# Encoding of the experts and their gates and decoders: from two turns of a loop to one written-out pipeline of 16 steps

## The reference, cut to what matters

```python
h = _ln(relu(x @ ew1 + eb1) @ ew2 + eb2, eg, ebeta)      # encoding
qkv = h @ aiw + aib                                      # encoding
...                                                      # attention, output projection,
hf = _lstm_dir(h, wif, whf, bf)                          # LSTM forwards and backwards
mem = concatenate([hf, hb])
gate_s = sigmoid(relu(mem @ sw1 + sb1) @ sw2 + sb2)      # gates
gate_t = tanh(relu(mem @ tw1 + tb1) @ tw2 + tb2)
g = gate_s * gate_t
out_e = _ln(relu(g @ dw1 + db1) @ dw2 + db2, dg, dbeta)  # decoder
...
out = einsum("ebsd,bse->bsd", outs, softmax(x @ router_w + router_b))
```

## Time and profile before

| | us |
|---|---|
| median of 3 runs | 5326.97 (5326.27 to 5326.97) |
| the profiled execution | 5325.8 |
| its span, first to last instruction | 5324.0 |
| encoding, from the memset of `evx` to the last store of `qk` | 289.35 to 622.77 |
| gates and decoders, from the first load to the last sum | 4773.99 to 5236.68 |
| PE busy, share of the span | 94% |
| DVE / ACT / POOL busy | 77% / 45% / 22% |

### The profile page before, as it was taken

The page is one execution under the profiler, slowest core; times in us unless marked ns, Lnnn a source line. Parts: engine busy times, 40 slices in busy tenths (PEclk is TensorE's granted clock), DMA queues, the critical chain, the costliest instruction groups (busy, mean ns, idle before and its releaser), DMA issues. The chain is left out here.

```text
span 5324.0 us, 258931 instructions
## 1 busy us (share of the span) xinstructions
PE 5025.1 (94%) x108704; PEld 3528.2 (66%) x108704; DVE 4120.1 (77%) x19249; ACT 2395.4 (45%) x8347; POOL 1150.2 (22%) x5133
## 2 busy tenths in 40 slices
PE   7978799999999996999999999999999999989895
PEld 4654433333333335999999999999999999974442
DVE  3855666666666658999999999999999999972225
ACT  2633465555555544444444444444444444433332
POOL 0000011111111101333333333333333333320000
PEclk9988899999999998999999999999999999999997
DMA  0023544545544441101111011110111011111200
GB/s 15 1 87 120 152 68 92 126 86 103 109 92 107 90 139 64 40 19 38 40 24 40 16 40 32 33 40 16 40 24 40 25 31 40 24 52 44 72 32 12
DMA packets 378774, 302.09 MB, mean 57 GB/s; under 512 B 146105, under 2 KB 357561, under 8 KB 372954
## 3 DMA queue, kind: packets, MB, share of 16 engines
q1 hardware_dynamic: 378382, 298.20, 23.4%
HBM read 179.14 MB, written 119.01 MB: 56 GB/s over the span
## 5 line engine op out<-in xcount | busy, mean ns | idle before, releaser
L1437 PE MATMUL bank<-lparts,lstate 128*32 128x256 bf16 x98304 | 2696.6, 273 | 55.1 <-PEq L1380 46.7
L1437 PEld LDWEIGHTS bank<-lparts,lstate 128*32 128x32 bf16 x98304 | 2461.6, 97 | 290.6 <-issue 47.5
L1448 DVE STREAM_TRANSPOSE ltz<-bank 128x256 f32<-128x256 f32 x2048 | 920.7, 450 | 8.3 <-PE bank L1437 3.8
L1512 ACT ACTIVATE ltc<-lgc 128x16 f32<-128x16 f32 x2049 | 443.1, 216 | 1030.0 <-DVE lgc L1469 1030.0
L1526 POOL TENSOR_TENSOR wh<-lgate,ltc 128x16 f32<-128x16 f32 x2052 | 471.6, 230 | 1798.3 <-ACT ltc L1512 1728.3
L1253 ACT ACTIVATE wh<-bank 128x512 f32<-128x512 f32 x1024 | 550.1, 600 | 482.9 <-PE bank L1040 482.3
L1165 DVE TENSOR_REDUCE bnegmax<-bank 128x1 f32<-128x512 f32 x1024 | 654.0, 682 | 130.7 <-PE bank L1022 130.4
L1507 ACT ACTIVATE lgate<-lz 128x48 f32<-128x48 f32 x2048 | 498.7, 244 | 520.8 <-DVE lz L1459 520.8
L1533 POOL COPY ltz<-wh 128x64 f32<-128x64 f32 x2048 | 603.2, 295 | 0.0
L1455 DVE TENSOR_TENSOR lhalf<-ltz 128x128 f32<-128x128 f32 x2048 | 582.1, 284 | 9.5 <-POOL ltz L1533 5.4
L1102 PE MATMUL bank<-xT,bw 128*128 128x512 f32 x1024 | 489.4, 602 | 2.7 <-DVE bzs L1186 1.9
(11 more groups left out here) (210 smaller groups left out, 4306.9 us busy)
## 6 DMA issues: line engine op xcount, KB each, us to landing
zx<-bzs SPq DMA_DIRECT2D x32, 2048.0 KB, 7.2
wh<-zx SPq DMA_DIRECT2D x64, 1024.0 KB, 7.5
qk<-eparts SPq DMA_DIRECT2D x96, 256.0 KB, 2.6
bqp<-qk SPq DMA_DIRECT2D x192, 128.0 KB, 4.8
bkp<-qk SPq DMA_DIRECT2D x192, 128.0 KB, 8.1
hs<-wh SPq DMA_DIRECT2D x32, 512.0 KB, 5.9
cmemT<-hs SPq DMA_DIRECT2D x32, 512.0 KB, 4.3
vx<-evx SPq DMA_DIRECT2D x16, 544.0 KB, 3.7
```

What stands on the lines that cost most here:

```text
L1437: last = nc.tensor.matmul(bank[x][32 * q:32 * q + 32, 0:256], top[:, x, e, k].rearrange("p m r -> p (m r)"), parts[:, way, g, k, n, e, q], ...
L1448: nc.vector.transpose(tz[:, x].rearrange("p (n w) -> p n w", w=SLOT)[:, :, 0:32], bank[x][:, 0:256].rearrange("p (n c) -> p n c", n=BLOCKS ...
L1512: nc.scalar.activation(tc[:, x], gc[:, x, 1], ACT.Tanh).then_inc(tanhed[x], 1)
```

## The change

In `experts_encode`:
- the loop over `turn` and its `clear_signals` are gone; 16 steps are written out in one block. The halves of the buffers are chosen by `s // B % 2`, the counters go on counting. The memset block stays;
- SP loads experts 0 and 1 at the head, expert 2 after the store of v of step 3, expert 3 after that of step 7;
- PE: encode1 of the next step now stands ahead of the transposes; encode2 of the next step is cut in two halves, one between the transposes and the k projection, one between the k and q projections;
- ACT: the relu of the next step stands ahead of `hT`.

In `experts_after`:
- the same writing-out, without loop and inner `clear_signals`; `wt` is filled for all four experts at the head;
- SP: the vectors of an expert are loaded behind `sw1` and `tw1`; experts 2 and 3 are loaded in steps 5 and 9, after `y_mm` and `summed` of steps 3 and 7;
- `y` goes to bank 2 (`Y_BANK`) instead of bank 4. The wait for `y_kept` moves from `hidden` to the first product of `gates`; `decode2` waits for the sigmoid of bank 2 in its place; `hidden` waits bank by bank for the relu of the step before; the second product of `gates` waits for `gate_kept`.

```diff
-        with nc.Fori(0, E // 2) as turn:
-            with nc.Block() as block:
...
+        with nc.Block() as block:
...
+                load_expert(0)
+                load_expert(1)
+                for b in range(steps):
...
+                    if b % B == B - 1 and b // B + 2 < E:
+                        load_expert(b // B + 2)
...
                 encode1(0)
+                for pair in range(2):
+                    encode2(0, pair)
                 for b in range(steps):
+                    if b < steps - 1:
+                        encode1(b + 1)
+                    turn_normed(b)
+                    if b < steps - 1:
+                        encode2(b + 1, 0)
+                    project(b, 1)
+                    if b < steps - 1:
+                        encode2(b + 1, 1)
+                    project(b, 0)
...
                 for b in range(steps):
+                    if b < steps - 1:
+                        relu(b + 1)
                     act.wait_ge(hn_turned, b + 1)
...
-            clear_signals(nc, [
-                qbs_done, h1_mm, h1_kept, h2_mm, h2_kept, stats_done, mv_done, var_done, std_done, rstd_done,
...
+    Y_BANK = 2
...
+                for s in range(2, STEPS):
+                    sp.wait_ge(hid_mm, 4 * (s - 1))
+                    load_states(s)
+                    if s % B == 1 and 1 < s // B + 1 < E:
+                        e = s // B + 1
+                        sp.wait_ge(y_mm, B * (e - 1))
+                        sp.wait_ge(summed, BT * B * (e - 1))
+                        load_expert(e)
...
                 def hidden(s):
                     pe.wait_ge(mem_in[s % 2], 32 * (s // 2 + 1))
-                        if s > 1:
-                            pe.wait_ge(y_kept, s - 1)
                     for m in range(4):
+                        if s > 0:
+                            pe.wait_ge(hid_kept, 4 * (s - 1) + m + 1)
...
                 def gates(s):
...
+                        if m == 0 and s > 1:
+                            pe.wait_ge(y_kept, s - 1)
+                        if m == 1 and s > 0:
+                            pe.wait_ge(gate_kept, 4 * (s - 1) + 2)
...
                 def decode2(s):
-                        pe.wait_ge(hid_kept, min(4 * (s + 1) + 1, 4 * STEPS_IN_TURN))
+                    pe.wait_ge(gate_kept, min(4 * (s + 1) + 1, 4 * STEPS))
```

More of the change, by code:

```diff
@@ L596, in experts_encode @@
     with ExitStack() as ctx:
-        steps = 2 * B
+        steps = E * B
         w = core.sb(ctx, "ew", [P, 2, ENC_W])
@@ L690, in encode2 @@
                         pe.wait_ge(h1_kept, 2 * b + 2)
                         if b % B == 0:
[L692 to L726, removed]
+                            pe.wait_ge(ew2_in[b // B % 2], 16 * (b // B // 2 + 1))
@@ new lines, in encode2 @@
+                    if b > 0:
+                        pe.wait_ge(h2_kept, 2 * (b - 1) + pair + 1)
+                    for t in (2 * pair, 2 * pair + 1):
+                        for k in range(KH):
+                            last = nc.tensor.matmul(bank[2 + pair][:, t % 2 * DM:(t % 2 + 1) * DM],
+                                                    h1[:, b % 2, k, t * P:(t + 1) * P],
+                                                    weight(b, "ew2", k, 0, DM), start=k == 0, stop=k == KH - 1)
@@ L727, in _, with project @@
+                def project(b, side):
+                    if side == 1:
                         pe.wait_ge(hT_kept, 2 * b + 2)
                         if b % B == 0:
[L729 to L740, removed]
@@ new lines, in _ @@
+                encode1(0)
+                for pair in range(2):
+                    encode2(0, pair)
+                for b in range(steps):
+                    if b < steps - 1:
[7 more added lines that the diff above has]
+                    project(b, 0)
+                    for pair in range(2):
+                        for t in (2 * pair, 2 * pair + 1):
+                            for k in range(KH):
+                                last = nc.tensor.matmul(bank[4 + pair][:, t % 2 * DM:(t % 2 + 1) * DM],
+                                                        hT[:, b % 2, k, t * P:(t + 1) * P],
+                                                        weight(b, "qkv", k, 2 * DM, DM), start=k == 0, stop=k == KH - 1)
+                        last.then_inc(v_mm, 1)
```

614 lines of the change are left out of this document (331 added, 283 removed).

## The result

The changed kernel took 5245.21 us (median, 5244.28 to 5246.02); the kernel before, run beside it, 5326.81. The ratio is 0.9846 with a 95% interval of 0.9835 to 0.9857: 1.5% faster, far outside the 0.2% that this kernel can tell from no change. Forecast were 5246 and a range of 5238 to 5264.

What follows compares the result with a forecast made beforehand. Encoding and gates were taken as bound by TensorE plus one wait a step. Terms -44.9, -32.5 and -3.5 sum to -80.9 us, from 5325.8 to 5244.9; with the median 1.2 above, forecast 5246, range 5238 to 5264.

Steps and rivals of the forecast that it cites:

- Part 1: Encoding, steady step: encode1 and half of encode2, moved, cover the waits for evx and ehT; period 17.45 to 16.45 us.
- rival (a): Encoding: relu or ehT arrives late, replacing the evx wait; period stays 17.45, total 5261 us; chance 9%.
- Part 2: Encoding, boundary between experts 1 and 2: drain and refill go, -28.6 us; whole stretch 291.7 to 246.8, -44.9.
- The -1.35 for step 0 to 1: Encoding's first interval between transposes, 17.77 us before, predicted to shorten by 1.35.
- Two of the signs I had named: Encoding: transposes 16.4 to 16.6 us apart through all steps; granted clock 1.00 from 311 us to the stage's end.
- Part 3: Gates, steady step: y in bank 2 meets the wait for cy; period 26.92 to 25.80 us.
- rival (c): Gates: bank 2 makes PE wait as bank 4 did, 14 x 1.1 us less gain, total 5261; chance 4%.
- Part 4: Gates, hidden of step 1 to 15: 393.7 to 361.2 us, -32.5; SP's moved loads stay hidden by 4 us.
- Part 5: Ends of both stages: in-loop clearing and loop's end go, -1.75 us each, -3.5 together.
- rival (b): Gates: states of steps 6 and 10 come late behind the weights, 2 x 9 us, total 5264; chance 5%.
- The lower sum: Ends of both stages: a fall-through exit saves only the clearing, about 1.1 us each, -2.2 together.
- Rival (d): Encoding: PE falls to the low clock around the transposes, 16.45 us more per step, up to 5509; chance 2%.

Runs made afterwards that it cites:

- experiment 2: The changed kernel with PE's new encoding order, but ScalarE's relu of the next step behind ehT again; a single execution took 5315.07 us.
- experiment 4: The kernel before, with both loops and inner clearings, but with the encoding's new step order and y in bank 2; 5299.45 us, ratio 0.9944.
- experiment 7: The changed kernel with useless matmuls in PE's idle times at the heads of both stages; 5242.83 us, ratio 0.984.
- experiment 3: The changed kernel with y in bank 4 again and the old wait at the head of hidden, still written out; 5259.55 us, ratio 0.987.
- experiment 6: The changed kernel with the weights of experts 2 and 3 loaded twice more ahead of the states of steps 6 and 10; 5256.75 us, ratio 0.9867.
- experiment 5: The changed kernel with four more empty blocks clearing the semaphores behind each of the two stages, eight in all; 5255.94 us, ratio 0.9863.

## Why the prediction was right, by its steps

**Part 1, steady step: right, with one more 0.09 us.** The meeting points came out as worked out. Counted from the start of encode1 (328.02), `evx` was taken at 0.90 (forecast 0.95), the relus ended at 2.61 (2.6) and PE wanted them at 2.67 (2.65), `ehT` was done at 4.25 (4.30) and wanted at 4.50 (4.37). VectorE's string from the k projection to `evx` took 12.9 us (13.0), and PE came for it at 13.76 (13.75). The period is 16.54, not 16.45; the 0.09 lies in the first half of encode2, which starts at 330.69, right behind the relu's end:

```profile
329.94 0.69 ACT L826 ACTIVATE eh<-bank,ecols 128x512 f32<-128x512 f32 x1 [0.17 <-PE bank L687]
330.82 1.45 ACT L852 ACTIVATE ehT<-bank,ecols 128x512 f32<-128x512 f32 x2 [0.18 <-PE bank L710]
```

The relu ends at 330.63, 0.06 us before encode2 starts, and encode2's first half takes 1.83 us to the next group's start where its second takes 1.73. In the kernel before, the same excess lay on the k projection, which started 0.07 us behind the end of `ehT`: 3.52 against the 3.44 of the q projection. After, with `ehT` ready 0.25 us ahead, both take 3.43. So it looks like the price of a product that is just in time, the tail of rival (a) at 0.1 us and not 1.0; no run moved the relu earlier to show it. Experiment 2 shows what the relu's place is worth: without its new place the same relu costs 2.7 us a step and the clock besides. The reason I gave for the new order holds, but I had not said what half of it would cost: the two orders are one change, and half of it is worse than none.

**Part 2, boundary: right in mechanism.** 45.07 became 16.54, and experiment 4 gives it to the writing-out. The forecast of the whole stretch, 246.8, missed by 2.4 us in three terms: the first interval was 18.42 and not 16.41 (+2.0, the low clock in step 0, which the prediction had left out); thirteen intervals of 16.54 (+1.2); the last 15.77 (-0.7), because step 14 issues its v and then no encode1 of a seventeenth step, which I overlooked. The -1.35 for step 0 to 1 is the one term with the wrong sign: 17.77 grew to 18.42. The low clock falls on encode2 or on this interval, a little differently in each kernel; with the clock up it is 16.81 (experiment 7). Two of the signs I had named failed with it: the granted clock was 0.91 and not 1.00 from 311 to 330 us, and the first and last intervals lay outside 16.4 to 16.6. And the window at 437 that I gave for the low clock of step 8 to 9 lies in the interval before it; the trace shows 0.80 and 0.77 from 479 to 487 us.

**Part 3, gates: right.** 25.82 against 25.80; the whole 1.1 us of bank 4 is gone, and by experiment 3 it comes back with the bank and its wait. That decides against rival (c).

**Part 4, boundary and SP's new order: right.** -32.2 against -32.5. The states landed 19.5 us into the step, forecast 21.5: the loads ran at up to 367 GB/s over 4 us, above the 241 on which the sum had been cautious. (The rows give the sums of step 3 at 5.5 us into the step and not 6.5; the first weights were issued at 6.6.) Experiment 6 shows the wait of rival (b) when the weights are tripled, 3.8 us.

**Part 5, ends: right in kind, too large.** 2.8 us and not 3.5. The 1.75 put the loop's end at 0.63 us beside a clearing of 1.12; experiment 5 leaves nothing for it. The lower sum that the prediction set beside it, -2.2, was the closer in mechanism, and 0.6 short, because the clearing behind the encoding costs 1.5 to 1.7 and not 1.12. The Trainium skill says (Runtime: NRT & Kernel Launch, Instruction fetch mechanics) that a taken branch out of the prefetched window makes an engine wait for code. The trace agrees with the half of it that the forecast used: an exit that falls through cost nothing visible. What the taken branch between the turns costs no run here separates.

**Rival (d)** did not come: 1.00 through the steady steps. But experiment 2 shows that the low clock is near, and the cover thin: a wait of 2.7 us behind the transposes was followed by the low clock in all steps but one.

**The sum.** Three steps fell short by 3.4 us together (2.4, 0.3 and 0.7), and stretches I had put at nothing gave 2.3 (the ledger's other rows): -79.8 of span against -80.9. That the miss was 1 us is partly luck, since these errors cancelled. 1.1 of the 2.3 lie at the gates' own head and not in the untouched stages. 0.3 of it, the way into the block, is 9.46 us in both kernels with loops and 9.18 or 9.19 in seven of the eight written-out ones (10.37 in experiment 2), so it goes with the writing-out. The other 0.8, first load to `hidden` 0, varies from 6.5 to 7.6 us among the written-out kernels, and its cause stays open.

## What to carry to other kernels

Where one wait a step stands on the bottleneck engine, put there work that depends on nothing of the step before, and reorder the engine that feeds it as well: here PE's new order with ScalarE's old one made the encoding 51 us longer than both old (316.06 against 264.73), and with ScalarE's new one 15 shorter. A boundary between two turns of a loop is worth its drain and refill, 27 us and 17 to 19 here, and only 1 to 2 us of it the clearing, by experiment 5's price. A wait behind transposes can cost twice: once itself, and once through the clock of what follows (41.7 and 25 us in experiment 2). A wait of 0.95 us ahead of them cost only itself.

## What the runs showed of the hardware that was not expected

- A wait of 2.7 us behind transposes left PE at the lower level (0.57 over 4 us) in 14 of 15 steps and cost about 25 us on top of its 41.7; a wait of 0.95 us beside the same transposes cost nothing of the clock. That the transposes are the reason, and not the wait alone, no run shows.
- A clearing of semaphores over an empty block costs 1.12 us in one place and 1.5 to 1.7 in another (experiment 5).
- The half of encode2 that starts right behind the end of its relu takes 0.1 us more than the other half (1.83 against 1.73), though the profile shows no idle time there, and so did the k projection before (3.52 against 3.44); why was not tried.
- Loads run at up to 367 GB/s over 4 us beside a PE that is never idle, and 3.9 MB passed at 390 (experiment 6), against the 241 of rows 9, which I had taken for the rate.
- Work that computes nothing pays in a head: nine matmuls ahead of the encoding's work and four ahead of the gates' took about 3 and 2 us off the work behind them, with the granted clock at 1.00 where it had been 0.52 and 0.50 (experiment 7). In the whole time the gain is not clear of the noise.
